# A decoder block with entmax attention: a quarter of the residuals and of the weights moved to POOL

## The reference, cut to what matters

```python
def entmax15(x):
    x = (x - jnp.max(x, -1, keepdims=True)) / 2.0
    ...                      # tau_star: the threshold for which the weights add up to 1
    return jnp.square(jnp.clip(x - tau_star, 0.0, None))

for _ in range(NUM_STEPS):                                   # 3 steps
    scores = jnp.einsum('bhsd,hnd->bhsn', xi, K) * beta      # 8 heads, 256 memory entries
    w = entmax15(scores)
    xi = jnp.einsum('bhsn,hnd->bhsd', w, V)
...
x = _layernorm(x + out @ Wo.T)
x = _layernorm(x + cross_attention(x, ctx))
x = _layernorm(x + dense(x))
```

## Time and profile before

| | |
|---|---|
| median of 3 runs | 892.58 us (891.53 to 894.0) |
| the profiled execution | 891.69 us |
| its span in the trace | 889.9 us |
| PE busy | 816.0 us, 92% |
| DVE busy | 770.2 us, 87% |
| ACT busy | 738.2 us, 83% |
| POOL busy | 493.2 us, 55% |
| PE's granted clock, mean over the span | 0.975 of full speed |

### The profile page before, as it was taken

One profiled execution on the slowest core, in us unless ns is written; L12 is line 12 of the kernel. 1 busy time (PEld: TensorE's weight loads), 2 busy tenths in 40 slices (PEclk: granted clock), 3 DMA queues, 4 the chain that ended last, 5 costly groups with the idle time before them and its releaser, 6 DMA issues.

```text
span 889.9 us, 18293 instructions
## 1 busy us (share of the span) xinstructions
PE 816.0 (92%) x5598; PEld 697.7 (78%) x5598; DVE 770.2 (87%) x1955; ACT 738.2 (83%) x1787; POOL 493.2 (55%) x2306
## 2 busy tenths in 40 slices
PE   7999998799999989999997999998999998998962
PEld 6878887588798878888876888787888877877751
DVE  4799998999999999989998999999899999996331
ACT  3599897989988999888899799989979899986420
POOL 4144446654565665676466656575675747765223
PEclk9999999899999989999999999999999999999986
DMA  8900120000000000000000000000000000000001
GB/s 279 212 1 1 37 72 4 12 5 7 1 1 1 2 1 1 1 3 1 26 0 1 11 13 1 1 2 1 2 22 2 1 20 1 8 1 1 2 1 33
DMA packets 24215, 17.63 MB, mean 20 GB/s; under 512 B 11760, under 2 KB 23536, under 8 KB 23856
## 3 DMA queue, kind: packets, MB, share of 16 engines
q1 hardware_dynamic: 23872, 16.13, 6.4%
q0 software_dynamic: 240, 0.27, 0.2%
HBM read 14.30 MB, written 2.10 MB: 18 GB/s over the span
## 4 chain that ended last, share of the span: by engine, by line
PE 52%; DVE 23%; ACT 15%; POOL 6%; issue 4%; DMA 0%; SPq 0%; POOLq 0%; DVEq 0%
PE banks L1257 20%; PE banks L1280 10%; DVE moments L816 9%; ACT work L726 6%; PE banks L1340 5%; PE banks L1268 5%; PE banks L1304 4%; DVE top L796 4%; PE banks L1128 3%; ACT work L717 3%; ACT work L738 2%; DVE work L836 2%; PE banks L1314 1%; ACT work L733 1%; PE banks L1332 1%
## 5 line engine op out<-in xcount | busy, mean ns | idle before, releaser
L816 DVE BATCH_NORM_STATS2 moments<-work 128x6 f32<-128x512 f32 x576 | 376.7, 687 | 8.0 <-ACT work L726 3.7
L726 ACT ACTIVATE work<-work,neg_u 128x256 f32<-128x256 f32 x768 | 334.2, 522 | 28.5 <-DVE neg_u L828 20.5
L1257 PE MATMUL banks<-weights_s,work 128*128 128x256 f32 x1536 | 352.9, 383 | 3.6 <-ACT work L717 2.4
L1257 PEld LDWEIGHTS banks<-weights_s,work 128*128 128x128 f32 x1536 | 286.8, 191 | 46.0 <-issue 7.0
L717 ACT ACTIVATE work<-banks,neg_low 128x256 f32<-128x256 f32 x384 | 155.9, 499 | 3.8 <-DVE neg_low L807 3.6
L948 POOL TENSOR_TENSOR resid_sum<-moments 128x8 f32<-128x8 f32 x144 | 30.3, 211 | 218.4 <-DVE moments L816 217.5
L796 DVE MAX8 top<-banks 128x8 f32<-128x256 f32 x384 | 140.6, 413 | 11.2 <-PE banks L1257 10.9
L1268 PE MATMUL banks<-ident,work 128*128 128x128 f32 x768 | 113.3, 283 | 21.1 <-ACT work L738 11.5
L738 ACT ACTIVATE work<-banks 128x512 f32<-128x512 f32 x192 | 113.6, 612 | 14.2 <-PE banks L1268 14.1
L1268 PEld LDWEIGHTS banks<-ident,work 128*128 128x128 f32 x768 | 90.4, 145 | 38.9 <-issue 20.4
L1280 PE MATMUL banks<-weights_s,work 128*128 128x256 f32 x512 | 115.9, 381 | 1.0 <-ACT work L738 1.0
(11 more groups left out here) (155 smaller groups left out, 1087.9 us busy)
## 6 DMA issues: line engine op xcount, KB each, us to landing
work<-in_L_xattn_Wo_dram SPq DMA_DIRECT2D x2, 1024.0 KB, 11.3
out_dram<-work SPq DMA_DIRECT2D x16, 128.0 KB, 1.8
work<-in_L_xattn_w_kc_q_dram SPq DMA_DIRECT2D x2, 768.0 KB, 5.5
...
```

The lines of the kernel that those rows point to most:

```text
L726: ins = nc.scalar.activation(q_resid[:, j, h, :], q_resid0[:, j, h, :], ACT.Relu, bias=small["neg_u"][:, j, h:h + 1])
L816: ins = nc.vector.bn_stats(moments[:, j, 2 * q:2 * q + 2, :].rearrange("p h k -> p (h k)"), r.rearrange("p h n -> p n h"))
L1257: ins = nc.tensor.matmul(ps_scores[:, h, :], lhsT, w[:, h, t, :], start=(t == 0), stop=(t == CT - 1))
```

## The change

Three constants and the stages behind them are changed. `DVE_WEIGHTS` goes from 2 to 1, and there are new constants `POOL_WEIGHTS = 1` and `POOL_RESID = 1`.

- Quarter 3 of `q_resid` of the second and third evaluation is made by POOL (`pool_resid`), with two TENSOR_SCALARs (add, then max with 0) of 128x256, and no longer by two ACTIVATEs.
- Of the weights, quarter 0 is on DVE, quarters 1 and 2 on ACT, and quarter 3 on POOL (`pool_weights`).
- The clip behind the third evaluation is gone: the weights are made from `neg_u_raw`, and DVE, ACT and POOL wait on `pool_step` in the place of `u_ready`. The clips of the first two evaluations stay.
- DVE's fourth `moments` of an evaluation and PE's fourth `turn_weights` now wait on POOL's count.
- All strings of `tile_turns()` are new.

```diff
-DVE_WEIGHTS = 2
+DVE_WEIGHTS = 1
+POOL_WEIGHTS = 1
+POOL_RESID = 1
...
         for e in range(EVALS):
-            dve += four("moments", s, e) + once("inverse", s, e) + once("clip", s, e)
-            act += four("resid", s, e) if e else []
+            dve += four("moments", s, e) + once("inverse", s, e)
+            dve += once("clip", s, e) if e < EVALS - 1 else []
+            act += four("resid", s, e)[:4 - POOL_RESID] if e else []
             pool += once("sums", s, e) + once("newton", s, e)
+            pool += four("pool_resid", s, e + 1)[4 - POOL_RESID:] if e < EVALS - 1 else []
         dve += four("weights", s)[:DVE_WEIGHTS]
-        act += four("act_weights", s)[DVE_WEIGHTS:] + four("square_weights", s)
+        act += four("act_weights", s)[DVE_WEIGHTS:4 - POOL_WEIGHTS] + four("square_weights", s)
+        pool += four("pool_weights", s)[4 - POOL_WEIGHTS:]
...
-        "POOL": "hh000010100212211112200022010110101222113332233233h2hhh000011101033300332322320112312144444333244002"
+        "POOL": "hh00000010100120221111211221222200022200101110102122021232033132313232132h3hhh0100301102100220102033032"
...
-            POOL_AT, POOL_PASS = (2, 12, 23), 37
+            POOL_AT, POOL_PASS = (2, 12 + POOL_RESID, 23 + 2 * POOL_RESID), 37 + 2 * POOL_RESID + POOL_WEIGHTS
...
+            def clip_count(p, s, e):
+
+                return p * (STEPS * (EVALS - 1)) + (s * (EVALS - 1) + e + 1)
+
+            def last_threshold(eng, p, j, s):
+
+                eng.wait_ge(pool_step[j], pool_count(p, s, EVALS - 1, 11))
+
...
-            RESID_STEP = EVALS * QUARTERS - DVE_WEIGHTS
+            ACT_RESID = QUARTERS - POOL_RESID
+            RESID_STEP = (EVALS - 1) * ACT_RESID + QUARTERS - DVE_WEIGHTS - POOL_WEIGHTS
...
                     elif stage == "act_weights":
 
-                        act.wait_ge(u_ready[j], eval_count(p, s, EVALS - 1))
+                        last_threshold(act, p, j, s)
                         for h in pair:
                             ins = nc.scalar.activation(q_resid[:, j, h, :], q_resid0[:, j, h, :], ACT.Relu,
-                                                       bias=small["neg_u"][:, j, h:h + 1])
+                                                       bias=small["neg_u_raw"][:, j, h:h + 1])
...
                         if e == 0:
                             dve.wait_ge(scores_used[j], quarter_count(p, s, q + 1))
+                        elif q < ACT_RESID:
+                            dve.wait_ge(resid_ready[j], resid_count(p, s, e, q + 1))
                         else:
-                            dve.wait_ge(resid_ready[j], resid_count(p, s, e, q + 1))
+                            dve.wait_ge(pool_step[j], pool_count(p, s, e - 1, 9 + e + q - ACT_RESID + 1))
...
                     elif stage == "weights":
-                        dve.wait_ge(u_ready[j], eval_count(p, s, EVALS - 1))
+                        last_threshold(dve, p, j, s)
                         for h in pair:
                             ins = nc.vector.tensor_scalar(q_resid[:, j, h, :], q_resid0[:, j, h, :],
-                                                          small["neg_u"][:, j, h:h + 1], 0.0, ALU.add, ALU.max)
+                                                          small["neg_u_raw"][:, j, h:h + 1], 0.0, ALU.add, ALU.max)
...
+                    elif stage == "pool_resid":
+
+                        pool.wait_ge(u_ready[j], clip_count(p, s, e - 1))
+                        if (p, j, s, e) == (0, 1, 0, 1):
+
+                            made_by(pool, "wo_t", 3)
+                        for h in (2 * q, 2 * q + 1):
+                            ins = nc.gpsimd.tensor_scalar(q_resid[:, j, h, :], q_resid0[:, j, h, :],
+                                                          small["neg_u"][:, j, h:h + 1], 0.0, ALU.add, ALU.max)
+                        ins.then_inc(pool_step[j], 1)
+                    elif stage == "pool_weights":
+
+                        last_threshold(pool, p, j, s)
+                        for h in (2 * q, 2 * q + 1):
+                            ins = nc.gpsimd.tensor_scalar(q_resid[:, j, h, :], q_resid0[:, j, h, :],
+                                                          small["neg_u_raw"][:, j, h:h + 1], 0.0, ALU.add, ALU.max)
+                        ins.then_inc(pool_step[j], 1)
...
                     elif stage == "turn_weights":
                         if q < DVE_WEIGHTS:
                             pe.wait_ge(weights_ready[j], p * (STEPS * DVE_WEIGHTS) + (s * DVE_WEIGHTS + q + 1))
+                        elif q < QUARTERS - POOL_WEIGHTS:
+                            pe.wait_ge(resid_ready[j], resid_count(p, s, EVALS, q - DVE_WEIGHTS + 1))
                         else:
-                            pe.wait_ge(resid_ready[j], resid_count(p, s, EVALS, q - DVE_WEIGHTS + 1))
+                            pe.wait_ge(pool_step[j], pool_count(p, s, EVALS - 1, 14 + q - (QUARTERS - POOL_WEIGHTS) + 1))
```

80 lines of the change are left out of this document (40 added, 40 removed).

## The result

The changed kernel takes 983.55 us (median of 4 runs, 981.66 to 984.91) against 893.29 us of the kernel before on the same chip (4 runs, 891.53 to 895.26). The ratio is 1.101, with a 95% interval of 1.098 to 1.103. Forecast were 878 us and a range of 861 to 898.

A forecast was written before the change was run, and what follows sets the result against it. ACT was taken as pacing the bad stretches, DVE hardly behind. By the chain -13.4 - 4.5 - 3 + 6 + 5 - 2 = -11.9 us, by the stretches -15; it took -14, so 878 us, range 861 to 898.

The forecast's parts named there:

- The work that leaves ACT and DVE: Residuals off ACT, 83.5 us, -13.4 on the path; weights and clips off DVE, 40.4 us, weights -4.5 on the path.
- The clip: Dropping the clip between `newton` and the weights removes a hop: -3 us (ends 0 and -11.1).
- What POOL takes: 288 new TENSOR_SCALARs of 128x256 at 0.55 us each; POOL's work grows by 158 us to 651 us, 73%.
- POOL's own queue: `sums` and `newton` behind the new pairs, and the queue blocked while `pool_resid` waits for a clip: +5 us (0 to +12).
- The ports: 304 exposed DVE instructions wait when they meet long POOL instructions: 22 us of DVE, +6 us (0 to +21).
- The clock: Fewer PE gaps, so less work at 1.2 GHz in 160 to 170 and 320 to 330 us: -2 us.
- The run-out: POOL's standstills of 5.83 and 7.43 us around `worst_all` near the end stay untouched: 0, plus or minus 2 us.
- B: POOL's long instructions slow the loop of the thresholds, DVE's waits 74 d squared: 902 us at d = 1.05, chance 0.22.
- A: The wait only changes its name, DVE being late wherever ACT was: 891 us (890 to 895), chance 0.13.
- C: PE alone is left, as all of ACT's waits and most of DVE's go: 855 to 861 us, chance 0.07.
- D: The change might not do what it says, which the counts of instructions would tell; given no chance.
- the signs named as proof of error: New POOL lines at 0.75 us or more, DVE's busy time not falling, PE's transposes waiting over 5 us for POOL.

The follow-up runs named there:

- cols64: Changed kernel, but each new POOL instruction makes only 64 of 256 columns (heads 6 and 7 partly computed, final test's limit lifted): 876.25 us, 0.982 of before.
- the columns: The runs cols64, cols128, cols192 and the control taken together, 64 to 256 columns per new POOL instruction: 876.25, 888.28, 930.61 and 982.56 us.
- cols128: Same as cols64, but with 128 of 256 columns for each new POOL instruction: 888.28 us, 0.996 of the kernel before.
- cols192: Same as cols64, but with 192 of 256 columns for each new POOL instruction: 930.61 us, 1.043 of the kernel before.
- the control: Same source as cols64 with all 256 columns on POOL and its other edits kept: 982.56 us, 1.102 of the kernel before.

## Why the prediction was wrong, point by point

**What bounds the kernel.** ACT and DVE as pacing engines: borne out. cols64, where the relief comes without the price, is 1.8% faster (2.0% to 1.5%), and PE's part of the chain goes from 52% to 75%.

**The work that leaves ACT and DVE.** L739 takes 250.5 us against 334.2, -83.7 where -83.5 was worked out; the weights on DVE 31.6 against 62.1, -30.5 where -31.1 was. ACT as a whole stands at 669.4 and not near 655, because a group's time can't be taken off an engine's as it is. Where one group's instruction follows another's their records overlap, and the groups of ACT add up to 824.3 us before and 732.6 now, 86.1 and 63.2 more than ACT's busy time. The work fell by 91.7 us, and 22.9 of it had been overlap. DVE stands at 748.4, where 750 was named as the sign; the same holds there (the groups fell by 34.1 us, the busy time by 21.8), so the agreement is in part luck.

**The clip.** -3 forecast, -3.3 measured (889.38 against 892.73 on the same chip; by the interval 0.5 to 4.2).

**What POOL takes: the step that failed first.** It put a piece at 0.55 us, with 0.44 and 1.05 as bounds; it takes 1.14, above both. The rows that gave the bounds were of other operations. A MEMSET's pace (1 ns for an element) and the small instruction's 0.20 us were put together as a floor, L1032 with twice the writes (1.05) was taken as the ceiling, and the add of the same shape (L1037, 0.73) as a neighbour from above because it reads more. At 128x256 the runs show that on POOL the operation sets the pace more than the number of inputs: 0.40 us for a copy, 0.72 for the add of two tensors, 0.92 for the add of a column as TENSOR_SCALAR, 1.14 with the second operation. No row of before held a TENSOR_SCALAR of POOL, so the upper bound had no ground, and the forecast gave the value near the lower one. The sentence of the Trainium skill that was set beside it (GPSIMD Engine Reference, § 4.1 Engine selection: one-input work roughly line-rate) leaned the same way. For the copy (0.40 us) the trace agrees with the estimate of 0.21 us and a fixed part; for the TENSOR_SCALAR, with one input just as well, it is off by a factor of almost three, and the measurement decides.

**POOL's own queue: the second step that failed.** It was sized at +5: the visits that meet a pair (21 us) and a third of the 62 us for which the queue was to stand blocked before a clip, times POOL's share of the chain before (11% of its busy time). The blocked queue did not come: POOL stands still for 2.5 us before L1009, and for 2.8 in cols64. The visits did. With 1.14 us a piece their formula gives 91 us, and by the 11% about +10, 8 more than at 0.51; the columns show +106 us of time for that step. The 11% was read from a kernel in which POOL was free 45% of the time, and it was held constant, while POOL's part of the chain grew from 2% to 64%.

The price put through the forecast's own sum shows how the two mistakes share the loss. The ports become +26 (96 us at 27%), the queue +12 (91 + 21 us at 11%), the sum +15 in place of -12, and the time about 908 us. So of the 106 us between forecast and result the price explains some 30, and the way in which a price acts through POOL's queue the other 76.

**The ports.** +6, from 22 us of DVE. At 0.51 us a piece the exposed groups are where they are without any new work (86.9 against 87.2 us), so the term is 0. At 1.14 the formula (74 d squared) gives 96 us, and 9 were measured. The earlier trace rows showed that a clip can wait for a whole POOL instruction; they did not show that every exposed instruction which meets one does. The formula took that for granted.

**The sum.** Near for a piece of 0.51 us (876.25 against 878), but in part by luck, because its errors cancel there: the costs of +6 and +5 are close to nothing at that price (no added DVE time; `inverse` waits 15.4 us for `step_den` against 13.4 before). With no costs to set against it, the 16.3 us that cols64 gains are what relief, clip and clock are worth together, where the sum had 22.9. The forecast's upper end, too, was narrower than its own terms: "0, so 890" is 892 by the base that it uses, and with the ends that it gives for the ports (+21) and the queue (+12) and none of the relief the sum reaches about 925. Even that is short of 984.

**The clock.** The forecast's sign is right where the relief comes alone: in cols64 the stretches from 160 to 170 and from 320 to 330 us are at full clock. At -2 it is too small to be told from the rest. In the changed kernel the mean granted clock is 0.956 of full speed, against 0.975, and PE is busy for 840.6 us with the same 5598 matmuls, 24.6 more: it stands still for 142.5 us in place of 73.9 and runs more of its work at the lower of the two levels (1.2 GHz).

**The run-out.** The changed kernel's POOL timeline, against the earlier trace rows:

```profile
958.82 0.38 POOL L1115 PARTITION_ALL_REDUCE worst_all<-worst  x1 [5.55 <-issue]
...
966.30 0.18 POOL L1026 TENSOR_TENSOR row_var<-row_mv,eps_col 128x1 f32<-128x1 f32 x1 [7.10 <-issue]
```

5.55 and 7.10 us in place of 5.83 and 7.43: 0, as forecast.

**The rivals.** B had the right sign and the right engine's instructions. It put the point from which it decides at 0.9 us; cols128 at 0.72 is still faster than before and cols192 at 0.93 already 4% slower, and a straight line between them crosses the time of before at 0.74. Its mechanism was DVE waiting at the ports, with 902 us at 1.05 us a piece. DVE's busy time went up by 15 us and not by 80; the queue, which B named only in its first sentence, does the work, and on the line between cols192 and the control 1.05 us a piece lies near 960. The rule of the Trainium skill that stood beside B (Perfetto Trace Analysis, § Optimizing Scalar/DVE Operations: such a move may not help, since the two engines share a port) agrees with the outcome here, but not with the reason. A, C and D are out: the time is near neither 891 nor 858, and the counts of instructions are as planned (L739 576, L1009 192, L1016 96). Of the signs named as proof of error two came (L1009 over 0.75 us; PE's transposes waiting 25.3 us for POOL), and the third, DVE's busy time, did not.
